# Mixture stage: GpSimd's bias addition at another unit, the output products over four units

## The chip, the core and the metric

The kernel runs on one core of a Trainium2 chip. The engines are TensorE (PE; its weight loads are shown apart as PEld), VectorE (DVE), ScalarE (ACT), GpSimd (POOL) and SyncE (SP), each with an instruction stream of its own; they wait for each other by semaphores. The metric is the device time of one execution in microseconds (us), the median of several runs.

## The reference, cut to what matters

Two transformer layers over 8 x 1024 tokens of width 256. Only the last part, the second layer's feed-forward, is touched: a mixture of 16 experts over 8 slices of 32 columns of each token.

```python
h = x @ Wm + bm
t = h.reshape(bs * L_ * H, HD)            # H = 8 slices, HD = 32
logits = t @ expert_emb
w = softmax(logits); topw, topi = top_k(w, 2)
hmid = gelu(einsum('td,edi->tei', t, W1) + b1)
eo = einsum('tei,eio->teo', hmid, W2) + b2
comb = (sel * topw[:, :, None]).sum(axis=1)   # the two chosen experts
out = comb.reshape(bs, L_, d)
return out @ Wo + bo                       # x + this is the result
```

The product with `Wo` is what is called the output product below, and `bo` is the bias that GpSimd adds to the residual tiles.

## The kernel before

`mixture_ffn` works through 16 blocks (m = 0 to 15) of 512 tokens, that is four tiles of 128 tokens each (t = 0 to 3). All experts are computed for all tokens, and gates that are zero for experts not chosen weigh them. A block has 32 units: `u = 16 * hc + e`, expert e on one half (hc) of the 8 slices. Each unit goes through a pipeline of four engines:

- PE `hidden` (L2010): four products of 512 columns into one of three pairs of banks, `HP`; a pair of them may start when ACT has emptied the pair that stood three pairs before.
- ACT (L2110): two gelus of 1024 elements for a unit.
- PE `expert_out` (L2020): the second product into the single bank `OP`. It waits for the gelus and for `y_ready`, that is until DVE has read the unit before.
- DVE `gate_unit` (L2207): adds the expert's bias, multiplies by the gates (`gates_spread`), and writes `gated` (two buffers), or `combined` itself where e is 0. It waits for `y_added`, so that POOL has finished with the buffer two units before.
- POOL `sum_up` (L2092): adds `gated` into `combined`. Where e is 0 it has nothing to add.

The order on every engine is written out by hand with tables that say what else a unit does. In unit u of block m, PE issues `hidden(u)`, `expert_out(u-1)`, then the output products of block m-1 that `OUTPUT_AT` names, then a piece of the front of block m+1 that `FRONT_AT` names. DVE follows with `gate_unit(u-1)`, the additions of those output products to the residual tiles (L2195), and its own pieces of the front. The front of the next block is: normalization `xn` (L2130) at units 0 and 1, two tiles each; transposes at units 2 to 5 (L1965, copied by L2135); the product with `Wm` at units 6 and 8 (L1971); logits at unit 10; maxima and the masks at 11 to 13; ACT's exponential after unit 14's gelus, with an activation table load before and after it; the reciprocal at 18 (L2172, L2174), gates at 19 and 20, and their transposes at 22. All products that are not `hidden` or `expert_out` share one bank, `MB` (`misc_bank`): each waits on `misc_free` until DVE has copied the one before.

POOL's stream for a block is one bias addition to the block's four residual tiles (L2081, 128 x 1024 elements) and then 30 additions of units. `let_front_pass` makes POOL's addition for unit u wait until a piece of the front that DVE does in unit u+1 is finished, for the pieces n, s, d, k and w; so the addition for unit 31 waits for the normalization at unit 0 of the next block. The bias addition has no such wait beyond one for the block's own normalization, which is long past except in block 0. DVE's first output addition of the block waits for it (`biased`).

The first block's front runs before the blocks; block 0 has no output products to issue, block 15 no front; the output products of block 15 come after the last unit. The two tables and the head of POOL's routine:

```python
FRONT_AT = dict(zip((0, 1, 2, 3, 4, 5, 6, 7, 8, 9, 10, 11, 12, 13, 18, 19, 20, 22), FRONT))
EXP_AT = 14
OUTPUT_AT = {15: (0, 1), 16: (2,), 17: (3,)}
```

Of the kernel before, what the change touches and what calls it, by code (L numbers as in the profile page):

```python
# [15 lines left out]
ALU = mybir.AluOpType  # L16
ACT = mybir.ActivationFunctionType
AX = mybir.AxisListType
P = 128
D = 256  # L20
# [1792 lines left out]
def mixture_ffn(nc, X, STATS, MEAN, RS, B, weights, out, ident):  # L1813
# [5 lines left out]
    TT = 4  # L1819
# [7 lines left out]
    with ExitStack() as ctx:  # L1827
# [3 lines left out]
        def sem(name):  # L1831
            return ctx.enter_context(nc.semaphore(name))

        wm, wo, w1s, w2, embd = weights.wm, weights.wo, weights.w1s, weights.w2, weights.embd
        bmc, b1c, b2c, bor = weights.bmc, weights.b1c, weights.b2c, weights.bor
# [31 lines left out]
        xn_ready = sem("xn2_ready")  # L1867
        biased = sem("biased2")
# [18 lines left out]
        ON_PE = "xhlg"  # L1887
        FRONT_AT = dict(zip((0, 1, 2, 3, 4, 5, 6, 7, 8, 9, 10, 11, 12, 13, 18, 19, 20, 22), FRONT))
        EXP_AT = 14
        OUTPUT_AT = {15: (0, 1), 16: (2,), 17: (3,)}  # L1890
        OUT_STORE_AT = 20
        STORE_AT = {5: (0,), 6: (1,)}
        LOAD_AT = {6: (0,), 7: (1,)}
# [64 lines left out]
        def _(pe):  # L1958
# [31 lines left out]
            def output(m, par, t, k):  # L1990
                if t == 0:
                    pe.wait_ge(y_added, NU * m + NU + 1)
                pe.wait_ge(misc_free, k + 1)
                for h in range(HC):
                    mm = nc.tensor.matmul(MB[:, 0:D], CM[:, par, h, t * P:(t + 1) * P], wo[:, h, :],  # L1995
                                          start=(h == 0), stop=(h == HC - 1))
                mm.then_inc(misc_done, 1)
# [16 lines left out]
            def expert_out(m, u):  # L2014
                hc, e = divmod(u, E)
                n = NU * m + u
                pe.wait_ge(y_ready, n + 1)
                pe.wait_ge(gelu_done, 2 * n + 2)
                for j in range(G):
                    mm = nc.tensor.matmul(OP[HD * j:HD * (j + 1), :], w2[:, e, :],  # L2020
                                          GH[:, (2 * u + j // 2) % 4, j % 2, :], start=True, stop=True,
                                          tile_position=(0, HD * j))
                mm.then_inc(o_done, 1)
# [3 lines left out]
            def one_block(m, par, first, last):  # L2027
                k = before(m)
                for u in range(NU):
# [5 lines left out]
                    elif not first:  # L2035
                        expert_out(m - 1, NU - 1)
                    for t in () if first else OUTPUT_AT.get(u, ()):
                        output(m - 1, 1 - par, t, k)
# [18 lines left out]
        @block.gpsimd  # L2057
        def _(pool):
            pool.sem_inc(y_added, 1)

            def let_front_pass(m, u):

                m, u = (m, u + 1) if u + 1 < NU else (m + 1, 0)
                if m >= NM - 1 or u not in FRONT_AT:
                    return
                part, t = FRONT_AT[u]
                if part == "n":
                    pool.wait_ge(xn_ready, TT * (m + 1) + 2 * t + 2)
                elif part == "s":
                    pool.wait_ge(slices_ready, HC * (m + 1) + t + 1)  # L2070
                elif part == "d":
                    pool.wait_ge(lm_ready, m + 2)
                elif part == "k":
                    pool.wait_ge(gates_kept, m + 2)
                elif part == "w":
                    pool.wait_ge(gates_ready, m + 2)

            def sum_up(m, par):
                pool.wait_ge(xn_ready, TT * (m + 1))
                xs = X[:, TT * m:TT * (m + 1), :]  # L2080
                nc.gpsimd.tensor_tensor(xs, xs, bor[:, :].unsqueeze(1).to_broadcast([P, TT, D]), ALU.add)\  # L2081
                  .then_inc(biased, 1)
                for u in range(NU):
                    hc, e = divmod(u, E)
                    n = NU * m + u
                    pool.wait_ge(y_ready, n + 2)
                    pool.wait_ge(y_added, n + 1)
                    if e == 0:
                        pool.sem_inc(y_added, 1)
                    else:  # L2090
                        let_front_pass(m, u)
                        nc.gpsimd.tensor_tensor(CM[:, par, hc, :], CM[:, par, hc, :], Y[:, u % 2, :], ALU.add)\  # L2092
                          .then_inc(y_added, 1)

            for m in range(NM):
                sum_up(m, m % 2)
# [27 lines left out]
        def _(dve):  # L2124
# [66 lines left out]
            def output(m, t, k):  # L2191
                if t == 0:
                    dve.wait_ge(biased, m + 1)
                dve.wait_ge(misc_done, k + 1)
                nc.vector.tensor_tensor(X[:, TT * m + t, :], X[:, TT * m + t, :], MB[:, 0:D], ALU.add)\  # L2195
                  .then_inc(misc_free, 1)

            def gate_unit(m, par, u):
                hc, e = divmod(u, E)
                n = NU * m + u  # L2200
                dve.wait_ge(o_done, n + 3)
                q, i = divmod(u, GE)
                if i == 0:
                    dve.wait_ge(gate_in[q % GGROUPS], 16 * G * (NG // GGROUPS * m + q // GGROUPS + 1))
                if e:
                    wait(dve, y_added, n)
                nc.vector.scalar_tensor_tensor(out=Y[:, u % 2, :] if e else CM[:, par, hc, :], in0=OP[:, :],  # L2207
                                               scalar=b2c[:, e:e + 1], in1=GS[:, q % GGROUPS, i, :], op0=ALU.add,
                                               op1=ALU.mult).then_inc(y_ready, 1)
# [4 lines left out]
            def one_block(m, par, first, last):  # L2214
                k = before(m)
                for u in range(NU):
                    if u >= 1:
                        gate_unit(m, par, u - 1)
                    elif not first:
                        gate_unit(m - 1, 1 - par, NU - 1)  # L2220
                    for t in () if first else OUTPUT_AT.get(u, ()):
                        output(m - 1, t, k)
# [34 lines left out]
def program(nc, a, out):  # L2257
    B = a["L0_attn_x"].shape[0]
    NT = B * KT
    with ExitStack() as ctx:  # L2260
        X = ctx.enter_context(nc.sbuf_tensor("x_tiles", [P, NT, D], F32))
        MEAN = ctx.enter_context(nc.sbuf_tensor("ln_mean", [P, NT], F32))
        RS = ctx.enter_context(nc.sbuf_tensor("ln_rstd", [P, NT], F32))
        STATS = ctx.enter_context(nc.sbuf_tensor("ln_stats", [P, NT, 6], F32))
        ident = ctx.enter_context(nc.sbuf_tensor("ident", [P, P], F32))
        identb = ctx.enter_context(nc.sbuf_tensor("ident_bf16", [P, P], BF16))
        make_idents(nc, ident, identb)
        causal_attention(nc, a["L0_attn_x"], X, STATS, MEAN, RS, B, a["L0_attn_Wq"], a["L0_attn_Wk"],
                         a["L0_attn_Wv"], ident, identb)
        expert_ffn(nc, X, STATS, MEAN, RS, B, *(a["L0_ffn_" + n] for n in (  # L2270
            "Wg", "bg", "Wu", "bu", "Wd", "bd", "Wq", "keys", "down_embed", "up_embed")), ident)
        later = MixtureWeights(nc, ctx, *(a["L1_ffn_" + n] for n in (
            "Wm", "bm", "expert_emb", "W1", "b1", "W2", "b2", "Wo", "bo")))
        rotary_attention(nc, X, STATS, MEAN, RS, B, *(a["L1_attn_" + n] for n in ("wq", "wk", "wv", "wo")),
                         a["rotation_cos"], a["rotation_sin"], ident, later)
        mixture_ffn(nc, X, STATS, MEAN, RS, B, later, out, ident)
# [32 lines left out]
```

## Time and profile before

| | us |
|---|---|
| median of 3 runs | 4446.77 (4442.31 to 4447.55) |
| the profiled execution | 4446.02 |
| its span, first to last instruction | 4444.3 |
| the mixture stage's blocks | from about 3138 to the end |
| one block in the middle of the stage | 80.88 |
| PE busy in such a block | 78.19 |
| ACT busy in such a block | 70.97 |
| DVE busy in such a block | 42.05 |
| POOL busy in such a block | 41.10 |

The rows further down are of four kinds. A row of busy time by stretch has the stretch in us from the span's start and its length, then the busy time and the count of instructions of PE, PEld, DVE, ACT and POOL, then TensorE's granted clock as a share of full speed, the busy share of the DMA engines and GB/s. A row of the chain of waits has a start, a length and the work. A row of waits has the waiting engine and line, the releaser, and total us, times and longest us. A row of the timeline has a start and a length in us, the engine, the line, what is written from what, shapes, and the number of instructions merged into it; in brackets stands how long the engine was idle before it and what ended that.

### The profile page before, as it was taken

Reading aid. Unit: us, or ns where it says so; the run is one execution under the profiler, and the core shown is the slowest. Engines: PE = TensorE matmul, PEld = TensorE weight load, DVE = VectorE, ACT = ScalarE, POOL = GpSimd, SP = SyncE. Lnnn points to the kernel's source line nnn. Section 1 sums busy time; section 2 is a strip of 40 time slices with the busy share of each in tenths; the row PEclk is TensorE's granted clock in tenths of the full one; section 3 lists DMA queues with packets and bytes.
Section 4 is the critical chain, followed back from the end, with each engine's and each line's share of the span. In section 5 each row is a group of like instructions: output and inputs, shape, how many; then the busy total and the mean of one; then the engine's idle time right before and its main releaser. Section 6 shows DMA issues by size and latency. Waiting matters only on the chain. (4 is left out here: it accounts for less than half of the span.)

```text
span 4444.3 us, 62551 instructions
## 1 busy us (share of the span) xinstructions
PE 4191.6 (94%) x22580; PEld 2204.3 (50%) x22580; DVE 2774.3 (62%) x5566; ACT 2654.1 (60%) x3193; POOL 1453.3 (33%) x1113
## 2 busy tenths in 40 slices
PE   7999999999978999999999998999899999999999
PEld 4444444444534566566565565555344444444443
DVE  6777777777748677677677655554455555554553
ACT  1555565565556454454454423444688888888888
POOL 3111111111125344343343322120354545545545
PEclk7999999999999999999999999999899999999999
DMA  7333433434210000000000001000766667666673
GB/s 174 83 95 81 101 75 79 97 91 84 60 56 1 0 1 1 1 1 1 1 1 1 0 1 33 1 1 1 165 140 163 154 140 164 152 151 162 140 163 92
DMA packets 145746, 322.79 MB, mean 73 GB/s; under 512 B 39296, under 2 KB 64272, under 8 KB 129056
## 3 DMA queue, kind: packets, MB, share of 16 engines
q1 hardware_dynamic: 137456, 310.88, 30.3%
q10 hardware_dynamic: 7920, 7.87, 0.6%
q8 instruction: 182, 2.98, 0.3%
q14 instruction: 124, 1.02, 0.1%
q0 software_dynamic: 64, 0.05, 0.0%
HBM read 237.93 MB, written 80.74 MB: 72 GB/s over the span
## 5 line engine op out<-in xcount | busy, mean ns | idle before, releaser
L2110 ACT ACTIVATE gelu_out<-hidden,b_col 128x1024 f32<-128x1024 f32 x1024 | 1084.2, 1112 | 160.8 <-PE hidden L2010 160.1
L648 DVE TENSOR_REDUCE maxima<-front 128x1 f32<-128x512 f32 (+3 forms) x1280 | 738.0, 631 | 175.5 <-PE front L458 101.6
L2092 POOL TENSOR_TENSOR combined<-combined,gated 128x512 f32<-128x512 f32 x480 | 619.6, 1291 | 664.7 <-DVE gated L2207 456.7
L550 ACT ACTIVATE probsT<-scoresT 128x1024 f32<-128x1024 f32 (+3 forms) x768 | 584.2, 812 | 305.7 <-PE scoresT L486 301.2
L1062 POOL TENSOR_TENSOR pair_sums<-sims 128x1024 f32<-128x1024 f32 x256 | 481.9, 1903 | 788.2 <-DVEq L1188 517.6
L2207 DVE SCALAR_TENSOR_TENSOR gated<-expert_out,b_col,gates_spread 128x512 f32<-128x512 f32 x480 | 360.0, 750 | 500.9 <-PE expert_out L2020 295.2
L2010 PE MATMUL hidden<-slice_stack,w_stack 128*128 128x512 f32 x2048 | 626.0, 427 | 15.0 <-ACT gelu_out L2110 15.0
L2020 PE MATMUL expert_out<-gelu_out,w_sb 128*32 128x512 f32 x4096 | 546.7, 606 | 24.7 <-DVE gated L2207 13.5
L2010 PEld LDWEIGHTS hidden<-slice_stack,w_stack 128*128 128x128 f32 x2048 | 351.4, 189 | 370.2 <-ACT gelu_out L2110 281.6
L399 POOL TENSOR_SCALAR_AFFINE_SELECT probsT<-probsT 128x512 f32<-128x512 f32 x256 | 163.4, 638 | 1078.7 <-ACT probsT L550 1078.7
L452 PE MATMUL front<-k_stack,q_stack 62*128 62x512 f32 (+3 forms) x1536 | 436.9, 429 | 34.8 <-DVE maxima L648 15.1
L452 PEld LDWEIGHTS front<-k_stack,q_stack 62*128 62x128 f32 x1536 | 216.9, 192 | 288.8 <-DVE maxima L648 183.9
L1117 ACT ACTIVATE pair_exp<-pair_sums,neg_max 128x1024 f32<-128x1024 f32 x256 | 284.5, 1116 | 120.4 <-DVE expert_weight L1218 114.2
L501 PE MATMUL pv<-probsT,values 128*32 128x512 f32 (+3 forms) x3072 | 332.4, 505 | 0.8 <-ACT outT L521 0.5
L1207 DVE SCALAR_TENSOR_TENSOR pair_exp<-pair_sums,top_pairs,pair_exp 128x1024 f32<-128x1024 f32 x256 | 322.3, 1281 | 11.1 <-ACT pair_exp L1117 10.9
L1194 DVE SCALAR_TENSOR_TENSOR hiddenT<-dense,bu_col,silu_gate 128x512 f32<-128x512 f32 x128 | 95.7, 750 | 366.0 <-PE dense L1012 366.0
L486 PE MATMUL scoresT<-q_stack,k_stack 64*128 64x512 f32 (+3 forms) x1536 | 304.6, 407 | 12.4 <-ACT probsT L550 9.5
L1100 ACT ACTIVATE silu_gate<-dense,bg_col 128x512 f32<-128x512 f32 x128 | 87.6, 687 | 305.2 <-PE dense L1004 305.1
L1218 DVE SCALAR_TENSOR_TENSOR expert_weight<-pair_exp,recip_z,expert_weight 128x1024 f32<-128x1024 f32 x192 | 246.5, 1284 | 8.4
L1004 PE MATMUL dense<-xnT,wg_sb 128*128 128x512 f32 x512 | 240.8, 592 | 2.2 <-ACT silu_gate L1100 2.1
L1012 PE MATMUL dense<-xnT,wu_sb 128*128 128x512 f32 x512 | 240.6, 592 | 0.0
L1028 PE MATMUL dense<-up_sb,silu_down 128*128 128x256 f32 x1024 | 231.8, 379 | 5.0 <-DVE silu_down L1243 5.0
(205 smaller groups left out, 5650.1 us busy)
## 6 DMA issues: line engine op xcount, KB each, us to landing
gates_spread<-gate_scratch SPq DMA_DIRECT2D x512, 256.0 KB, 4.8
stack_scratch<-split_parts SPq DMA_DIRECT2D x192, 256.0 KB, 3.0
slice_stack<-slice_scratch SPq DMA_DIRECT2D x128, 256.0 KB, 7.7
q_stack<-stack_scratch SPq DMA_DIRECT2D x64, 384.0 KB, 6.2
k_stack<-stack_scratch SPq DMA_DIRECT2D x64, 384.0 KB, 9.3
slice_scratch<-slice_parts SPq DMA_DIRECT2D x32, 512.0 KB, 6.2
out_x<-x_tiles ACTq DMA_DIRECT2D x15, 512.0 KB, 5.0
x_tiles<-in_L_attn_x SPq DMA_DIRECT2D x7, 1024.0 KB, 11.8
```

The costliest lines, as they stand in the source:

```text
L452: mm = nc.tensor.matmul(F[k % 3][:, a * w:at], QS[rows, hf, q, qt * P:(qt + 1) * P], KS[rows, hf, q, kc * BANK:kc * BANK + w], start=True, ...
L486: mm = nc.tensor.matmul(bank[:, e, at:BANK], KS[rows, hf, q, kt * P:(kt + 1) * P], QS[rows, hf, q, c * BANK + at:(c + 1) * BANK], start=Tr ...
L501: mm = nc.tensor.matmul(PV[32 * j:32 * (j + 1), at:BANK], V[:, n % 2, kt, (G * g + j) * HV:(G * g + j) * HV + 32], PT[:, i % NPT, j, at:BA ...
L550: nc.scalar.activation(PT[:, i % NPT, 2 * pr:2 * pr + 2, at:BANK], ST[pr][:, :, at:BANK], ACT.Exp, scale=SCALE).then_inc(probs_ready, 1)
L648: nc.vector.tensor_reduce(dst, F[k % 3][:, 0:parts * w].rearrange("p (a k) -> p a k", a=parts), AX.X, ALU.max)\
L1062: nc.gpsimd.tensor_tensor(A[:, h, :].rearrange("p (i j) -> p i j", i=NR), SM[:, m % 2, t, 0, h, 0:NR].unsqueeze(2).to_broadcast([P, NR, NK ...
L1207: nc.vector.scalar_tensor_tensor(out=E[h % 2][:, :], in0=A[:, h, :], scalar=T8[:, H * t + h, TOPK - 1:TOPK], in1=E[h % 2][:, :], op0=ALU.i ...
L2010: mm = nc.tensor.matmul(HP[k % HPB][:, j, :], w1s[:, e, :], HS[:, par, G * hc + 2 * p + j, :], start=True, stop=True)
L2020: mm = nc.tensor.matmul(OP[HD * j:HD * (j + 1), :], w2[:, e, :], GH[:, (2 * u + j // 2) % 4, j % 2, :], start=True, stop=True, tile_positi ...
L2092: nc.gpsimd.tensor_tensor(CM[:, par, hc, :], CM[:, par, hc, :], Y[:, u % 2, :], ALU.add)\
L2110: nc.scalar.activation(GH[:, k % 4, :, :], HP[k % HPB][:, :, :], ACT.Gelu, bias=b1c[:, u % E:u % E + 1])\
L2207: nc.vector.scalar_tensor_tensor(out=Y[:, u % 2, :] if e else CM[:, par, hc, :], in0=OP[:, :], scalar=b2c[:, e:e + 1], in1=GS[:, q % GGROU ...
```

## The change

Two places. POOL's bias addition for block m is no longer issued ahead of the block's units but just ahead of its 27th unit (u = 26, `BIAS_AT`), with the same wait and the same semaphore. And the output products of the four tiles, with DVE's additions that follow them, are issued one each at units 15, 16, 17 and 18, where they were two at 15 and one each at 16 and 17. No instruction is added or removed.

```diff
-        OUTPUT_AT = {15: (0, 1), 16: (2,), 17: (3,)}
+        BIAS_AT = 26
+        OUTPUT_AT = {15: (0,), 16: (1,), 17: (2,), 18: (3,)}
...
             def sum_up(m, par):
-                pool.wait_ge(xn_ready, TT * (m + 1))
-                xs = X[:, TT * m:TT * (m + 1), :]
-                nc.gpsimd.tensor_tensor(xs, xs, bor[:, :].unsqueeze(1).to_broadcast([P, TT, D]), ALU.add)\
-                  .then_inc(biased, 1)
                 for u in range(NU):
                     hc, e = divmod(u, E)
                     n = NU * m + u
+                    if u == BIAS_AT:
+                        pool.wait_ge(xn_ready, TT * (m + 1))
+                        xs = X[:, TT * m:TT * (m + 1), :]
+                        nc.gpsimd.tensor_tensor(xs, xs, bor[:, :].unsqueeze(1).to_broadcast([P, TT, D]), ALU.add)\
+                          .then_inc(biased, 1)
                     pool.wait_ge(y_ready, n + 2)
                     pool.wait_ge(y_added, n + 1)
```

POOL's stream at a border between two blocks, before (the additions for units 19 to 31, then the bias addition of the next block, then its unit 1):

```order
L2092 TENSOR_TENSOR combined<-combined,gated 128x512 [waits gates_ready,y_added,y_ready]
L2092 TENSOR_TENSOR combined<-combined,gated 128x512 [waits y_added,y_ready] x11
L2092 TENSOR_TENSOR combined<-combined,gated 128x512 [waits xn2_ready,y_added,y_ready]
L2081 TENSOR_TENSOR x_tiles<-x_tiles,bo_rows 128x1024 [waits xn2_ready]
L2092 TENSOR_TENSOR combined<-combined,gated 128x512 [waits y_ready,y_added]
```

The same place in the changed kernel (its L2094 is L2092 of before, L2086 is L2081):

```order
L2094 TENSOR_TENSOR combined<-combined,gated 128x512 [waits gates_ready,y_added,y_ready]
L2094 TENSOR_TENSOR combined<-combined,gated 128x512 [waits y_added,y_ready] x6
L2086 TENSOR_TENSOR x_tiles<-x_tiles,bo_rows 128x1024 [waits xn2_ready]
L2094 TENSOR_TENSOR combined<-combined,gated 128x512 [waits y_added,y_ready] x5
L2094 TENSOR_TENSOR combined<-combined,gated 128x512 [waits xn2_ready,y_added,y_ready]
L2094 TENSOR_TENSOR combined<-combined,gated 128x512 [waits y_ready,y_added]
```

The bias addition has moved from between units 31 and 1 to between units 25 and 26. No wait has gone or come.

PE's stream in units 15 to 19, from the `expert_out` issued in unit 15, before (L1995 is an output product, two instructions for a tile):

```order
L2020 MATMUL expert_out<-gelu_out,w_sb 32x512 x4
L1995 MATMUL misc_bank<-wo_sb,combined 128x256 x4
L2010 MATMUL hidden<-slice_stack,w_stack 128x512 x4
L2020 MATMUL expert_out<-gelu_out,w_sb 32x512 x4
L1995 MATMUL misc_bank<-wo_sb,combined 128x256 x2
L2010 MATMUL hidden<-slice_stack,w_stack 128x512 x4
L2020 MATMUL expert_out<-gelu_out,w_sb 32x512 x4
L1995 MATMUL misc_bank<-wo_sb,combined 128x256 x2
L2010 MATMUL hidden<-slice_stack,w_stack 128x512 x4
L2020 MATMUL expert_out<-gelu_out,w_sb 32x512 x4
L2010 MATMUL hidden<-slice_stack,w_stack 128x512 x4
```

The same stretch in the changed kernel (L1996, L2011 and L2021 are L1995, L2010 and L2020 of before):

```order
L2021 MATMUL expert_out<-gelu_out,w_sb 32x512 x4
L1996 MATMUL misc_bank<-wo_sb,combined 128x256 x2
L2011 MATMUL hidden<-slice_stack,w_stack 128x512 x4
L2021 MATMUL expert_out<-gelu_out,w_sb 32x512 x4
L1996 MATMUL misc_bank<-wo_sb,combined 128x256 x2
L2011 MATMUL hidden<-slice_stack,w_stack 128x512 x4
L2021 MATMUL expert_out<-gelu_out,w_sb 32x512 x4
L1996 MATMUL misc_bank<-wo_sb,combined 128x256 x2
L2011 MATMUL hidden<-slice_stack,w_stack 128x512 x4
L2021 MATMUL expert_out<-gelu_out,w_sb 32x512 x4
L1996 MATMUL misc_bank<-wo_sb,combined 128x256 x2
L2011 MATMUL hidden<-slice_stack,w_stack 128x512 x4
```

In unit 15 one tile's output product follows `expert_out` where there were two, and unit 18, which had none, has the fourth tile's.

## Rows read from the trace of the kernel before

**Rows 1.** Busy time by stretch, block 1 to 2; columns are explained above
```profile
3321.47:3402.35 80.88, 78.19 (x437) 33.87 (x437) 42.05 (x90) 70.97 (x68) 41.10 (x31) 1.00 0.66 152
```

**Rows 2.** Chain of waits, the same product (unit 6) in blocks 0, 1, 2
```profile
3161.45 1.91 PE misc_bank L1971 x4
...
3240.60 1.91 PE misc_bank L1971 x4
...
3321.47 1.91 PE misc_bank L1971 x4
```

**Rows 3.** Waits on PE, blocks 1 to 14: us in total, times, longest
```profile
PE expert_out L2020 <- DVE gated L2207: 12.6, 14, 0.9
```

**Rows 4.** Timeline, units 1 to 5 of block 4; columns are explained above
```profile
3471.68 2.88 DVE L2130 TENSOR_SCALAR xn<-x_tiles,ln_mean,ln_rstd 128x256 f32<-128x256 f32 x2
3471.71 2.38 POOL L2081 TENSOR_TENSOR x_tiles<-x_tiles,bo_rows 128x1024 f32<-128x1024 f32 x1
...
3473.20 1.18 PE L2010 MATMUL hidden<-slice_stack,w_stack 128*128 128x512 f32 x4
...
3475.28 1.06 PE L2020 MATMUL expert_out<-gelu_out,w_sb 128*32 128x512 f32 x8 [0.90 <-DVE gated L2207]
...
3476.47 1.18 PE L2010 MATMUL hidden<-slice_stack,w_stack 128*128 128x512 f32 x4
...
3478.76 1.18 PE L2010 MATMUL hidden<-slice_stack,w_stack 128*128 128x512 f32 x4
```

**Rows 5.** Timeline, unit 0 of block 5, normalization with no bias addition beside it
```profile
3550.44 0.73 DVE L2130 TENSOR_SCALAR xn<-x_tiles,ln_mean,ln_rstd 128x256 f32<-128x256 f32 x2
```

**Rows 6.** Timeline, units 15 to 20 of block 4
```profile
3509.40 4.13 ACT L2110 ACTIVATE gelu_out<-hidden,b_col 128x1024 f32<-128x1024 f32 x4
...
3511.67 1.06 PE L2020 MATMUL expert_out<-gelu_out,w_sb 128*32 128x512 f32 x8 [0.36 <-ACT gelu_out L2110]
...
3513.44 1.28 PE L2010 MATMUL hidden<-slice_stack,w_stack 128*128 128x512 f32 x4
...
3516.43 1.28 PE L2010 MATMUL hidden<-slice_stack,w_stack 128*128 128x512 f32 x4
...
3516.82 0.42 DVE L2195 TENSOR_TENSOR x_tiles<-x_tiles,misc_bank 128x256 f32<-128x256 f32 x1 [0.28 <-PE misc_bank L1995]
...
3518.64 1.20 PE L2010 MATMUL hidden<-slice_stack,w_stack 128*128 128x512 f32 x4
...
3520.19 0.35 DVE L2174 RECIPROCAL gate_recip<-gate_recip 128x32 f32<-128x32 f32 x1
...
3520.76 1.20 PE L2010 MATMUL hidden<-slice_stack,w_stack 128*128 128x512 f32 x4
3520.90 0.75 DVE L2207 SCALAR_TENSOR_TENSOR gated<-expert_out,b_col,gates_spread 128x512 f32<-128x512 f32 x1 [0.35 <-POOL combined L2092]
```

**Rows 7.** Timeline of PE, unit 16 of block 0, no output products
```profile
3188.79 0.74 PE L2010 MATMUL hidden<-slice_stack,w_stack 128*128 128x512 f32 x2 [2.33 <-ACT gelu_out L2110]
3189.89 1.06 PE L2020 MATMUL expert_out<-gelu_out,w_sb 128*32 128x512 f32 x8 [0.36 <-ACT gelu_out L2110]
```

**Rows 8.** Timeline, late units of block 4
```profile
3541.23 1.28 POOL L2092 TENSOR_TENSOR combined<-combined,gated 128x512 f32<-128x512 f32 x1 [0.85 <-DVE gated L2207]
...
3542.52 0.75 DVE L2207 SCALAR_TENSOR_TENSOR gated<-expert_out,b_col,gates_spread 128x512 f32<-128x512 f32 x1 [1.37 <-POOL combined L2092]
...
3544.65 0.75 DVE L2207 SCALAR_TENSOR_TENSOR gated<-expert_out,b_col,gates_spread 128x512 f32<-128x512 f32 x1 [1.37 <-POOL combined L2092]
```

**Rows 9.** Timeline, unit 0 of block 15, bias addition beside a gating instruction
```profile
4360.61 2.40 POOL L2081 TENSOR_TENSOR x_tiles<-x_tiles,bo_rows 128x1024 f32<-128x1024 f32 x1
4360.66 0.75 DVE L2207 SCALAR_TENSOR_TENSOR combined<-expert_out,b_col,gates_spread 128x512 f32<-128x512 f32 x1 [1.37 <-PE expert_out L2020]
```

**Rows 10.** Timeline of PE, unit 15 of block 15
```profile
4390.25 1.13 PE L1995 MATMUL misc_bank<-wo_sb,combined 128*128 128x256 f32 x4
4391.96 1.13 PE L1995 MATMUL misc_bank<-wo_sb,combined 128*128 128x256 f32 x4 [0.58 <-DVE x_tiles L2195]
```

## The prediction, made before the changed kernel ran

> **What bounds the kernel now.** I read the chain of waits first. From 3138 us on it is PE work almost alone, and the same product comes back in it every 80.87 us; from block 0 to block 1 it is 79.15 [rows 2]. A block is thus a fixed cycle, and a step counts if it lengthens that cycle. The busy time by stretch says how tight the cycle is: PE is busy 78.19 of 80.88 us, ACT 70.97, DVE and POOL about half, and the granted clock is 1.00, the upper of the two levels, 2.4 GHz [rows 1]. So DVE and POOL matter only where one of them makes PE or ACT late at a certain unit. The timeline then shows where. An ordinary unit takes 2.12 us (the gating instructions of two units in a row start at 3542.52 and 3544.65) [rows 8], about the time of its two gelus: four of them take 4.13 us [rows 6]. A unit with a transpose takes 2.29 (3476.47 to 3478.76) [rows 4]. Two places stand out, and the change touches both: units 2 to 3, and units 15 to 17.
>
> **Part 1: the bias addition leaves the block's start.** At unit 1 DVE normalizes two tiles and POOL starts the bias addition in the same moment. The pair of normalizations takes 2.88 us [rows 4]; at unit 0 the same pair takes 0.73 [rows 5]. DVE is held for 2.15 us, nearly the 2.38 us of the addition. The next gating instruction queues behind the normalization on DVE, and `expert_out` waits for that one: PE is idle for 0.90 us before it, and the unit lasts 3.27 us (3473.20 to 3476.47) where the next lasts 2.29, a loss of 0.98 us [rows 4]. The waits on PE have this 14 times, 12.6 us in all [rows 3]: in the starts of blocks 1 to 14. Block 0's bias addition ran in the prologue, beside nothing that it held, and block 15 has no normalization beside it.
>
> With the addition gone from there POOL has nothing between the additions for units 31 and 1, so nothing can hold the normalization. The gating instruction then waits for `expert_out` alone, as in other units, and the unit falls to its neighbours' 2.29. The next thing that is late there is PE itself. **Term 1: 14 x 0.98 = 13.7 us less.**
>
> **Part 1, the other end: the addition in unit 26.** No piece of the front lies in units 23 to 31, so DVE does only gating there. Two things could cost time.
>
> (a) The addition could hold a gating instruction as it held the normalization. In these units an addition of POOL ends (3541.23 + 1.28 = 3542.51) when the next gating instruction starts (3542.52) [rows 8], so the bias addition will start together with a gating instruction and cover it. The trace has just this case: in block 15 the bias addition runs from 4360.61 to 4363.01 and the gating instruction that starts at 4360.66 takes 0.75 us, as everywhere [rows 9]. Nothing is held. Here the Trainium skill speaks against the change: its page "SBUF — State Buffer", section "SBUF: two separate sides", says that a VectorE instruction in a two-port mode or with two SBUF inputs and a GpSimd instruction exclude each other for the whole instruction. The gating instruction reads the gates and the bias column from SBUF, and if the column counts as the second input it would be held in unit 26. That is a rival below; rows 9 speak against it, and by them the price is nothing.
>
> (b) The additions behind it are late. Bias addition 2.38 and addition of unit 26 1.28, from 3542.51 in the frame of rows 8, end at 3546.2. Who waits for it is the gating of unit 28, two gating starts later, at 3542.52 + 2 x 2.12 = 3546.77. That leaves some 0.5 us, and from there POOL, with 1.28 us of work for a unit of 2.12, catches up. Cost taken: nothing; cover: 0.5 us of slack, plus what PE has behind DVE.
>
> Where the addition's end is awaited (DVE's first output addition, a dozen units into the next block) it is early in either place.
>
> **Part 2: the output products.** What do the four products cost now? Block 0 has none, and from its unit 6 to the next block's it takes 79.15 us; the next stretch, with four products, takes 80.87 [rows 2]. Four products cost 1.72 us together. In units 16 and 17, the hidden products start 2.99 us apart (3513.44 to 3516.43) where ordinary units take 2.12 [rows 6], so each of these two costs 0.87, and 2 x 0.87 = 1.74 is already all of it: **the two products in unit 15 are free.** The reason is in the same rows: ACT, which has loaded its table for the exponential and loaded gelu's again, starts the gelus of unit 15 only at 3509.40, and `expert_out` in unit 16 waits for the second of them until 3511.67, idle for 0.36 before [rows 6]. In block 0, without products, PE is idle for 2.33 us in that place [rows 7]. Both products fit into that gap.
>
> So taking one product out of unit 15 brings nothing in blocks 1 to 14: `expert_out` of unit 16 still waits for the same gelu. The product of tile 1 goes to unit 16 and that of tile 2 to 17, where others stood, and the fourth goes to unit 18. Units 18 and 19 (hidden products at 3516.43, 3518.64, 3520.76) take 2.21 and 2.12 [rows 6]; the 2.21 is the echo of the product before it. ACT has no lead there that could hide a product. I take for unit 18 what units 16 and 17 pay, 0.87. **Term 2: 14 x 0.87 = 12.2 us more.** Bounds: nothing, if unit 18 had a gap, and 0.35 more if DVE became late. On DVE the fourth output addition stands ahead of the reciprocal pair, which now ends at 3520.54. An output addition waits 0.28 and takes 0.42 [rows 6], so the pair ends 0.70 later, at 3521.24, and the next gating instruction, due at 3520.90 + 0.87 = 3521.77, has 0.5 us to spare. The wait of 0.35 before it goes. Hence no extra.
>
> Block 15 has no exponential, so no gap in unit 15. There the second product starts 1.71 us after the first, with a wait of 0.58 for DVE to empty the bank [rows 10]. Moved to a unit of its own, it costs 0.87: **Term 3: 1.71 - 0.87 = 0.84 us less**, once.
>
> The shorter work of PE in unit 15 leaves it idle for about 2.33 less one product's 0.87, some 1.5 us. Block 0's 2.33 us of idle were followed by `expert_out` at 1.06 us, the ordinary time [rows 7], so the clock stays up.
>
> **The sum.** -13.7 + 12.2 - 0.8 = -2.4 us. A middle block goes from 80.88 to 80.77. Against the profiled execution's own 4446.02 that is 4443.6; the median of the runs, 4446.77, less 2.4 is 4444.4. I say **4444**.
>
> **Rivals.**
>
> *The fourth product is free as well* (faster). If PE had a gap in unit 18, or the freed 0.98 us early in the block gave ACT a lead that lasts, term 2 would go: -13.7 - 0.8 = -14.5, 4431.5 us. For it: the change shortens the crowd in unit 15. Against it: units 18 and 19 already run at the gelus' pace with no idle time, and the table loads end any lead.
>
> *The gap in units 2 to 3 stays* (slower). The hold of the normalization could come from POOL's addition for unit 31, which stands right ahead of the bias addition on POOL, or the 0.90 us could have another cause that only now shows. Then term 1 is nothing: 4446.0 + 12.2 - 0.8 = 4457.4. Against it: at unit 0 there is no bias addition and the pair takes 0.73.
>
> *The gating instruction is held in unit 26* (much slower). Place: the gating that starts with the bias addition; price: up to the addition's 2.38 us, in 16 blocks, up to 38 us on top of 4443.6, so up to 4482. It decides from the point where that instruction takes more than 0.75 us, or where the additions behind come over 0.5 us later than in (b). Rows 9 exclude it as far as one case can.
>
> **How the numbers follow.** Forecast 0.84; fourth product free 0.07; gap stays 0.06; gating held 0.03. The range takes the forecast with its bounds: upward 14 x 0.35 = 4.9 us, 4448.5, and a little for the spread of the runs (5 us from lowest to highest), 4450; downward half of term 2 and the spread, 4436. It leaves the three rivals out, 0.16 together. About 0.2%, 8.9 us, is what a measurement can tell from no change: faster means below 4437.9, slower above 4455.7. Faster: 0.07 and 0.02 of the forecast, 0.09. Slower: 0.06 + 0.03, 0.09. Same: the other 0.82.
>
> **What would show it.** Step 1: the normalization pair at unit 1 takes 0.73 to 0.8, and the 14 waits of `expert_out` for the gating, 12.6 us, are gone. Step 1b: bias additions between units 25 and 26, gating instructions at 0.75 throughout, hidden products 2.12 apart in units 24 to 31. Step 2: three units of 2.99 (16, 17 and 18) in place of two, the gelus of unit 15 and `expert_out` behind them no earlier relative to the block, PE idle over 1 us in unit 16 before its second pair. The block 80.77 long; block 15 shorter by 0.8. I would be wrong if unit 18 stayed near 2.12, if a gating instruction near the bias addition took over 0.75, or if the first units kept a unit of 3.27.

## The result, and the profile after

The changed kernel takes 4459.25 us (median of 8 runs, 4451.48 to 4464.62), the kernel before 4446.5 (8 runs, 4442.0 to 4449.72). The ratio is 1.003, 95% interval 1.002 to 1.0039: **slower by 0.3%, 12.8 us**, where 4444 was forecast, with 4450 as the upper end. Its runs also lie wider apart, 13 us where the kernel before has 8.

The chain of waits of the changed kernel, the same product in unit 6 of blocks 1 to 5 (start, length, work), to be read beside [rows 2]:

```profile
3242.86 1.91 PE misc_bank L1972 x4
...
3323.64 1.91 PE misc_bank L1972 x4
...
3404.41 1.91 PE misc_bank L1972 x4
...
3486.78 1.91 PE misc_bank L1972 x4
...
3569.20 1.92 PE misc_bank L1972 x4
```

The blocks are no longer alike. Two take 80.78 and 80.77 us, to the hundredth what was forecast, and the next two 82.37 and 82.42. Of the 13 such stretches from block 1 to block 14, seven last 80.77 or 80.78 us and six 82.31 to 82.42; with block 14's own there are seven long blocks: 3, 4, 8, 10, 11, 13 and 14.

PE in units 15 to 17 of block 4, a long block (columns as in the timeline of before: start, length, engine, line, work, instructions, idle time before it):

```profile
3511.05 1.13 PE L1996 MATMUL misc_bank<-wo_sb,combined 128*128 128x256 f32 x4
3511.83 0.82 PE L2011 MATMUL hidden<-slice_stack,w_stack 128*128 128x512 f32 x2
3514.12 0.73 PE L2011 MATMUL hidden<-slice_stack,w_stack 128*128 128x512 f32 x2 [1.47 <-ACT gelu_out L2112]
3515.22 1.67 PE L2021 MATMUL expert_out<-gelu_out,w_sb 128*32 128x512 f32 x8 [0.36 <-ACT gelu_out L2112]
3516.82 2.08 PE L1996 MATMUL misc_bank<-wo_sb,combined 128*128 128x256 f32 x4
3518.33 1.57 PE L2011 MATMUL hidden<-slice_stack,w_stack 128*128 128x512 f32 x4
...
3521.61 1.28 PE L2011 MATMUL hidden<-slice_stack,w_stack 128*128 128x512 f32 x4
```

The same place in block 5, a short one:

```profile
3594.24 0.82 PE L2011 MATMUL hidden<-slice_stack,w_stack 128*128 128x512 f32 x2
3596.53 0.74 PE L2011 MATMUL hidden<-slice_stack,w_stack 128*128 128x512 f32 x2 [1.47 <-ACT gelu_out L2112]
3597.63 1.07 PE L2021 MATMUL expert_out<-gelu_out,w_sb 128*32 128x512 f32 x8 [0.36 <-ACT gelu_out L2112]
...
3599.41 1.28 PE L2011 MATMUL hidden<-slice_stack,w_stack 128*128 128x512 f32 x4
...
3602.39 1.28 PE L2011 MATMUL hidden<-slice_stack,w_stack 128*128 128x512 f32 x4
```

Up to `expert_out` (L2021) the two are the same: one output product (L1996), half of `hidden`, 1.47 us idle for ACT, the other half, 0.36 us idle. Then `expert_out` takes 1.67 us instead of 1.07 and the next output product 2.08, where that of unit 15 took 1.13. From the second half of `hidden` to the `hidden` of unit 18 it is 7.49 us against 5.86: 1.63 us lost. The six long stretches exceed the others by 1.54 to 1.65 us. The busy time by stretch of the long block says why (stretch and length; busy time of PE, PEld, DVE, ACT, POOL; granted clock; DMA share; GB/s):

```profile
3512.00:3515.50 3.50, 1.67 (x9) 0.68 (x11) 0.42 (x1) 3.49 (x4) 1.28 (x1) 1.00 1.06 289
3515.50:3519.00 3.50, 3.50 (x13) 1.83 (x6) 0.82 (x2) 1.58 (x2) 1.24 (x1) 0.51 0.78 156
```

For one stretch of about 3.4 us the granted clock is 0.51, the lower of the two levels, 1.2 GHz, and before it PE was busy for 1.67 of 3.5 us. In the kernel before no such stretch lies in blocks 1 to 14; here there are seven, one in each long block, and each begins in this place, between 28.4 and 29.3 us behind the start of the block's product of unit 6. Below, such a stretch of half clock in unit 16, or just ahead of it, is called a fall.

A thin PE is not the whole of it. In the same 3.5 us of block 5 (3594.41 to 3597.91) PE is busy for 1.67 too, and the granted clock stays at 1.00. In the kernel before, the same place of block 4 has two output products, an idle time of 0.58 us between them and none before `hidden`, and PE is busy for 2.56 of 3.5 us:

```profile
3509.21 1.13 PE L1995 MATMUL misc_bank<-wo_sb,combined 128*128 128x256 f32 x4 [0.58 <-DVE x_tiles L2195]
3509.99 1.32 PE L2010 MATMUL hidden<-slice_stack,w_stack 128*128 128x512 f32 x4
```

and, by stretch, with the columns as above,

```profile
3508.45:3511.95 3.50, 2.56 (x13) 1.54 (x16) 0.84 (x2) 3.49 (x4) 1.27 (x1) 1.00 1.06 269
```

The rest of the change went as its parts were meant. DVE and POOL at the block's start, where [rows 4] had 2.88 us for the pair of normalizations:

```profile
3474.08 0.73 DVE L2132 TENSOR_SCALAR xn<-x_tiles,ln_mean,ln_rstd 128x256 f32<-128x256 f32 x2
3475.55 0.75 DVE L2209 SCALAR_TENSOR_TENSOR combined<-expert_out,b_col,gates_spread 128x512 f32<-128x512 f32 x1 [0.73 <-PE expert_out L2021]
3476.21 0.73 DVE L2132 TENSOR_SCALAR xn<-x_tiles,ln_mean,ln_rstd 128x256 f32<-128x256 f32 x2
3477.67 0.75 DVE L2209 SCALAR_TENSOR_TENSOR gated<-expert_out,b_col,gates_spread 128x512 f32<-128x512 f32 x1 [0.73 <-PE expert_out L2021]
```

Both pairs take 0.73, and the 14 waits of `expert_out` for the gating, 12.6 us [rows 3], are gone: among the waits on PE in blocks 1 to 14 only ACT is left. The first row below holds 14 waits of 1.47 us in unit 16 and 13 of 0.84 us near the block's end, which the kernel before has too.

```profile
PE hidden L2011 <- ACT gelu_out L2112: 31.5, 27, 1.5
PE expert_out L2021 <- ACT gelu_out L2112: 5.0, 14, 0.4
```

And the bias addition in its new place, unit 26 of block 4, with the gating beside it and hidden products 2.12 us apart:

```profile
3544.27 2.40 POOL L2086 TENSOR_TENSOR x_tiles<-x_tiles,bo_rows 128x1024 f32<-128x1024 f32 x1
...
3546.32 1.20 PE L2011 MATMUL hidden<-slice_stack,w_stack 128*128 128x512 f32 x4
3546.45 0.75 DVE L2209 SCALAR_TENSOR_TENSOR gated<-expert_out,b_col,gates_spread 128x512 f32<-128x512 f32 x1 [1.37 <-PE expert_out L2021]
3546.61 4.16 POOL L2094 TENSOR_TENSOR combined<-combined,gated 128x512 f32<-128x512 f32 x3
...
3548.44 1.20 PE L2011 MATMUL hidden<-slice_stack,w_stack 128*128 128x512 f32 x4
```

The gating takes 0.75 us as everywhere; POOL's next three additions run in a row (4.16 us), and nobody waits for them.

The profiled execution took 4459.2 us with a span of 4457.5, against 4446.02 and 4444.3 before. The 13.2 us between the spans are made of:

| | us |
|---|---|
| units 2 and 3 of blocks 1 to 14, 14 x 0.98 | -13.7 |
| fourth product in unit 18 of blocks 1 to 14, 14 x 0.87 | +12.2 |
| block 15, from its unit 15 to 20: 14.07 us instead of 14.92 | -0.85 |
| half clock in unit 16 of seven blocks, 7 x 1.63 | +11.4 |
| first of the last output products at half clock, 2.07 instead of 1.13 | +0.94 |
| ahead of the mixture stage, whose code is the same | +3.2 |
| sum | +13.2 |

The 3.2 us ahead of the stage belong to no change: the stage's first transpose starts at 3113.31 us where it was 3110.01, and over the ten profiles of this document, whose code up to there is the same, it starts between 3106.1 and 3113.9.

### The profile page after: what moved, and what is told of

Same layout as the page of the kernel before. It is cut to its first block and busy times, and to the rows that moved or that the text cites. A ratio compares the mean times of both kernels' runs of the same rounds, so it can differ in the third digit from the quotient of the medians.

```text
span 4457.5 us, 62551 instructions
## 1 busy us (share of the span) xinstructions
PE 4204.3 (94%) x22580; PEld 2212.0 (50%) x22580; DVE 2745.8 (62%) x5566; ACT 2653.1 (60%) x3193; POOL 1450.6 (33%) x1113
## 5 line engine op out<-in xcount | busy, mean ns | idle before, releaser
L2094 POOL TENSOR_TENSOR combined<-combined,gated 128x512 f32<-128x512 f32 x480 | 618.9, 1289 | 734.6 <-DVE gated L2209 509.7
L2011 PE MATMUL hidden<-slice_stack,w_stack 128*128 128x512 f32 x2048 | 633.5, 430 | 35.5 <-ACT gelu_out L2112 35.5
L2021 PE MATMUL expert_out<-gelu_out,w_sb 128*32 128x512 f32 x4096 | 550.2, 609 | 12.0 <-ACT gelu_out L2112 5.7
L2011 PEld LDWEIGHTS hidden<-slice_stack,w_stack 128*128 128x128 f32 x2048 | 354.9, 190 | 383.3 <-ACT gelu_out L2112 293.0
```

Of the source, the lines that this page charges most:

```text
L2011: mm = nc.tensor.matmul(HP[k % HPB][:, j, :], w1s[:, e, :], HS[:, par, G * hc + 2 * p + j, :], start=True, stop=True)
```

## The experiments

Theory 1: the single output product of unit 15 leaves PE too thin in the time in which it waits for ACT's table loads, and TensorE's clock falls behind that wait. Theory 2: the bias addition in unit 26 costs, by itself or through the clock. All times are medians beside the kernel before on the same chip.

### Each part alone

The bias addition moved, the products as before (against the changed kernel):

```diff
-        OUTPUT_AT = {15: (0,), 16: (1,), 17: (2,), 18: (3,)}
+        OUTPUT_AT = {15: (0, 1), 16: (2,), 17: (3,)}
```

> The bias addition in unit 26, the output products as before (two in unit 15, one each in 16 and 17). Theory 1 (the thinner unit 15 lets TensorE's clock fall behind the wait for the gelus): this part alone is a pure gain, 14 x 0.98 = 13.7 us, about 4432.5, blocks of 79.90 us, no stretch of half clock in blocks 1 to 14. Theory 2 (the bias addition beside the gating in unit 26 is what costs, by its own time or by the clock): not faster than before, 4446 or more, and half-clock stretches or units over 2.12 us near unit 26.

Measured: 4431.6 us (4428.07 to 4437.58, 8 runs) beside 4444.37 of before, ratio 0.9971 (0.996 to 0.9981). Unit 6 of blocks 1 and 2 in the chain of waits:

```profile
3241.81 1.91 PE misc_bank L1972 x4
...
3321.72 1.91 PE misc_bank L1972 x4
```

79.91 us, and all 13 such stretches last 79.90 to 79.92. There is no half clock in blocks 1 to 14. **The first part alone makes the kernel faster by 12.8 us**, and theory 2 is out.

The products moved, the bias addition at the block's start (against the kernel before):

```diff
-        OUTPUT_AT = {15: (0, 1), 16: (2,), 17: (3,)}
+        OUTPUT_AT = {15: (0,), 16: (1,), 17: (2,), 18: (3,)}
```

> The output products one each in units 15 to 18, the bias addition at the block's beginning. Theory 1: about seven blocks of 14 lose 1.6 us to half clock in unit 16, and the fourth product costs 0.87 in each: 4446 + 12.2 - 0.8 + 7 to 9 x 1.63, about 4470; the unit of 3.27 us is back. Theory 2: blocks of 81.75 us and no half clock, about 4457.

Measured: 4460.67 us (4456.71 to 4461.29, 5 runs), ratio 1.0032 (1.0019 to 1.0046). Blocks without a fall last 81.73 to 81.75 us, the forecast 81.75; in the profiled run three of blocks 1 to 14 (1, 5 and 14) hold a fall, and the stretches of the first two last 83.3. So the clock falls with the products alone, but three times where I had expected seven to nine: the median is 9 us under my figure. The wait is the same as with the whole change. In block 1, where the clock fell:

```profile
3266.79 0.73 PE L2010 MATMUL hidden<-slice_stack,w_stack 128*128 128x512 f32 x2 [1.46 <-ACT gelu_out L2110]
3267.89 1.14 PE L2020 MATMUL expert_out<-gelu_out,w_sb 128*32 128x512 f32 x8 [0.36 <-ACT gelu_out L2110]
3268.97 2.08 PE L1995 MATMUL misc_bank<-wo_sb,combined 128*128 128x256 f32 x4
3270.48 2.06 PE L2010 MATMUL hidden<-slice_stack,w_stack 128*128 128x512 f32 x4
```

How thin PE is in that place bears on whether the clock can fall; it does not alone decide how often.

### PE given more to do in the wait

The changed kernel, where in blocks 1 to 14 the product of unit 15 is computed twice over, into the same place:

```diff
+                for again in range(2 if t == 0 and m < NM - 2 else 1):
+                    for h in range(HC):
...
-                for h in range(HC):
```

> The changed kernel, but in unit 15 of blocks 1 to 14 the one output product is done twice over (four matmul instructions in place of two, the same result): TensorE does more work in the place where two products stood before. Theory 1: the added work lies in the wait for the gelus and costs nothing, the idle time before the second half of hidden falls from 1.47 to about 0.7 us, no half clock in blocks 1 to 14, all blocks 80.77 us, about 4443.5, so faster than the changed kernel by more than 10 us. Rival: if the clock has another cause, the time stays at about 4459, or rises by up to 14 x 0.78 = 11 us.

Measured: 4443.65 us (4440.48 to 4449.42, 10 runs), ratio 0.9998 (0.9989 to 1.0008), and not one stretch of half clock in the blocks. PE in units 15 and 16 of block 4:

```profile
3503.62 1.99 PE L1997 MATMUL misc_bank<-wo_sb,combined 128*128 128x256 f32 x8
3505.26 0.82 PE L2012 MATMUL hidden<-slice_stack,w_stack 128*128 128x512 f32 x2
3506.69 0.74 PE L2012 MATMUL hidden<-slice_stack,w_stack 128*128 128x512 f32 x2 [0.61 <-ACT gelu_out L2113]
3507.78 1.06 PE L2022 MATMUL expert_out<-gelu_out,w_sb 128*32 128x512 f32 x8 [0.36 <-ACT gelu_out L2113]
```

The idle time is down from 1.47 to 0.61 us, and `expert_out` starts no later against the gelus (0.36 idle before it, as ever). All blocks from the first on last 80.76 to 80.78. Work that nobody needs makes the changed kernel faster by more than 10 us, and it lands where the prediction had put the changed kernel, at 4443.6.

With half of that filler, one matmul instruction more than the changed kernel (the timeline counts each of these instructions as two, so 6 where there were 4):

```diff
+                for hs in ((0,), range(HC)) if t == 0 and m < NM - 2 else (range(HC),):
+                    for h in hs:
...
-                for h in range(HC):
```

> The changed kernel with one matmul instruction more in unit 15 (three in place of two; the second filler had four): PE's idle time falls from 1.47 to about 1.1 us. Theory 1: fewer falls of the clock than with the change, between none and four of 14 blocks, 4443.5 to 4452. If only a full product's work keeps the clock up, as many falls as with the change: about 4459.

Measured: 4443.91 us (4440.54 to 4446.58, 10 runs), ratio 0.9993 (0.9984 to 1.0003). The wait:

```profile
3506.97 1.56 PE L1997 MATMUL misc_bank<-wo_sb,combined 128*128 128x256 f32 x6
3508.19 0.82 PE L2012 MATMUL hidden<-slice_stack,w_stack 128*128 128x512 f32 x2
3510.05 0.73 PE L2012 MATMUL hidden<-slice_stack,w_stack 128*128 128x512 f32 x2 [1.04 <-ACT gelu_out L2113]
3511.14 1.07 PE L2022 MATMUL expert_out<-gelu_out,w_sb 128*32 128x512 f32 x8 [0.36 <-ACT gelu_out L2113]
```

1.04 us idle, and no fall in any block (80.76 to 80.78 us throughout). I had left room for up to four. Some 0.4 us of matmul work in that place separate seven falls, or the five of the second profile below, from none.

### Less to do in the wait, and no wait at all

The products in units 16 to 19, none in 15:

```diff
-        OUTPUT_AT = {15: (0,), 16: (1,), 17: (2,), 18: (3,)}
+        OUTPUT_AT = {16: (0,), 17: (1,), 18: (2,), 19: (3,)}
```

> The changed kernel with the four products in units 16, 17, 18 and 19, none in 15: the idle time before the second half of hidden grows from 1.47 to about 2.3 us. Without any fall of the clock a block is 81.6 us and the kernel 4443.6 + 13 = 4456.5. Theory 1: half clock in at least as many blocks as with the change (7 of 14), rather in most of them: 4468 to 4480. Rival (idle time is not what counts; block 0 had 2.33 us of it twice without a fall): no more falls than with the change, 4456 to 4468.

Measured: 4470.68 us (4469.67 to 4476.64, 4 runs), ratio 1.006 (1.0045 to 1.0075). Blocks without a fall last 81.63 or 81.64 us. Nine of blocks 1 to 14 hold falls (2, 3, 4, 7, 8, 9, 12, 13 and 14), and block 0 too; blocks 2, 7 and 12 hold one twice as long and last 84.1. One such block:

```profile
3518.51 0.74 PE L2011 MATMUL hidden<-slice_stack,w_stack 128*128 128x512 f32 x2
3521.58 1.22 PE L2011 MATMUL hidden<-slice_stack,w_stack 128*128 128x512 f32 x2 [2.33 <-ACT gelu_out L2112]
3522.73 1.94 PE L2021 MATMUL expert_out<-gelu_out,w_sb 128*32 128x512 f32 x8
```

2.33 us idle, and here already the second half of `hidden` runs at half clock, 1.22 us instead of 0.74. The fall is as frequent as theory 1 wanted, and no longer confined to what follows the wait. Block 0 is the very place of [rows 7], with the same code and the same 2.33 or 2.34 us of idle time, and here the granted clock is 0.50 (3193.50 to 3196.80): `expert_out` takes 1.94 us (at 3194.70) where [rows 7] has 1.06.

The wait itself taken away: ACT computes a square in place of the exponential, and the trace has no table load beside it. The gates, and with them the result, are then not the reference's.

```diff
-                nc.scalar.activation(EX[:, :, :, :], LM[:, :, :, :], ACT.Exp).then_inc(ex_ready, 1)
+                nc.scalar.activation(EX[:, :, :, :], LM[:, :, :, :], ACT.Square).then_inc(ex_ready, 1)
```

> The changed kernel with ACT's exponential replaced by a square, which needs no table load (the gates are then not the reference's): the cause of TensorE's wait is gone, not the wait filled. Theory 1: the idle time of 1.47 us in unit 16 goes, no half clock in blocks 1 to 14, a block is 80.77 - 2.17 = 78.60 us (the stretch from hidden to expert_out of unit 15 falls to block 15's 4.12 from 6.29), about 4413. Rival (the falls come from something else in the new order): half clock stays in some blocks, 1.6 us each, about 4425.

Measured: 4411.76 us (4407.61 to 4414.36, 4 runs), ratio 0.992 (0.9905 to 0.9935), all blocks 78.59 or 78.60 us, no half clock in blocks 1 to 14. PE goes straight from the output product to the whole of `hidden` and to `expert_out`:

```profile
3499.12 1.13 PE L1996 MATMUL misc_bank<-wo_sb,combined 128*128 128x256 f32 x4
3499.90 1.28 PE L2011 MATMUL hidden<-slice_stack,w_stack 128*128 128x512 f32 x4
3501.11 1.06 PE L2021 MATMUL expert_out<-gelu_out,w_sb 128*32 128x512 f32 x8
```

With the order of the changed kernel but without the wait nothing falls. The table loads cost a block 2.17 us here, 30 us in blocks 1 to 14 together.

### The changed kernel once more

> The changed kernel once more, beside the others on one chip. Theory 1: falls of the clock again, each in unit 16, in a number that differs from run to run, so a median between 4451 and 4465 and a spread wider than before's; blocks without one are 80.77 us again. If the falls of the first profile were a chance of one chip: about 4443.6 and none.

Measured: 4457.08 us (4444.45 to 4461.96, 10 runs) beside 4445.55 (4441.64 to 4450.45, 19 runs), ratio 1.0023 (1.0014 to 1.0032). Its profiled run took 4451.05 us and has five falls, in blocks 8, 10, 11, 13 and 14, all in unit 16; the other blocks last 80.76 to 80.78. By the sum, 4443.6 + 5 x 1.63 = 4451.8. One of the ten runs, 4444.45, is as fast as if the clock had not fallen at all. The mean granted clock of the single runs goes the same way: 0.978 in the run of 4444.45, as in most runs of the kernel before, and 0.974 in that of 4461.96. So the number of falls is what spreads the changed kernel's times, as far as a mean over the whole run can show it.

### A version that fills the wait with needed work

If 2.3 us of PE's time are free in that place, all four output products should go there. A second pair of products needs a second bank; `expert_out`'s is free between DVE's gating of unit 14 and `expert_out` of unit 15. Each pair fills a bank and DVE adds it in one instruction; the bias addition stays in unit 26. PE's part of the edit (DVE's additions, the stores and the semaphore counts are adapted to pairs, not shown):

```diff
-        OUTPUT_AT = {15: (0,), 16: (1,), 17: (2,), 18: (3,)}
+        OUTPUT_AT = {15: (0, 1)}
...
+                else:
+                    pe.wait_ge(y_ready, NU * (m + 1) + (16 if m < NM - 1 else 1))
+                bank = OP if t else MB
+                for i in range(2):
+                    for h in range(HC):
+                        mm = nc.tensor.matmul(bank[:, D * i:D * i + D], CM[:, par, h, (2 * t + i) * P:(2 * t + i + 1) * P],
+                                              wo[:, h, :], start=(h == 0), stop=(h == HC - 1))
...
+                    if u - 1 == max(OUTPUT_AT) and not first:
+                        pe.wait_ge(misc_free, k + 1)
```

> A version that uses the wait for the gelus in unit 15 in full: bias addition in unit 26, and all four output products in unit 15, two tiles into the bank of the front's products and two into expert_out's bank (free there between the gating of unit 14 and expert_out of unit 15), each pair with one DVE addition of 128 x 512. If two products in unit 15 are free because PE waits there for 2.33 us, four products (4 x 0.78 = 3.1 us) overrun it by little and the 1.74 us a block that two products still cost go: blocks of 78.2 to 78.5 us, 4404 to 4409 us, no half clock in blocks 1 to 14. If DVE's reading of the second bank makes expert_out late, each block keeps up to 1 us of it: up to 4420.

Measured: **4410.05 us** (4406.41 to 4413.19, 4 runs) beside 4445.55, ratio 0.9917 (0.9902 to 0.9931): 0.8% faster than the kernel before and the best of all. No half clock in blocks 1 to 14. Units 15 and 16 of a block:

```profile
3495.76 1.99 PE L2002 MATMUL misc_bank<-wo_sb,combined 128*128 128x256 f32 x8
...
3497.60 1.89 PE L2002 MATMUL expert_out<-wo_sb,combined 128*128 128x256 f32 x8
3497.67 2.12 ACT L2120 ACTIVATE gelu_out<-hidden,b_col 128x1024 f32<-128x1024 f32 x2
...
3499.14 1.28 PE L2017 MATMUL hidden<-slice_stack,w_stack 128*128 128x512 f32 x4
3499.52 0.69 DVE L2207 TENSOR_TENSOR x_tiles<-x_tiles,expert_out 128x512 f32<-128x512 f32 x1 [0.97 <-PE expert_out L2002]
3499.99 9.61 ACT L2120 ACTIVATE gelu_out<-hidden,b_col 128x1024 f32<-128x1024 f32 x9 [0.20 <-PE hidden L2017]
...
3500.34 1.07 PE L2027 MATMUL expert_out<-gelu_out,w_sb 128*32 128x512 f32 x8
```

The eight matmuls that the timeline counts for each pair follow each other, ACT starts its gelus at 3497.67 in the middle of them, and its idle time is 0.20 us. The price of the second bank is there too: `expert_out` starts only when DVE has read it, at 3500.34, 0.55 us after the end of the first two gelus. A block lasts 78.61 us (3235.70 to 3314.31, unit 6 of blocks 1 and 2 in the chain of waits) where I had put 78.2 to 78.5. Of the 1.74 us that two products cost, 1.3 are gained (79.91 with the bias addition moved alone, 78.61 here).

## Why the prediction was wrong

**What held.** Term 1 was right: 0.98 us in each of 14 blocks, shown by the blocks of 79.91 us with the bias addition moved alone, forecast by the same working at 79.90. The addition in unit 26 costs nothing: the gating beside it takes 0.75 us and PE's pace stays at 2.12. So the row of block 15 [rows 9] was the right guide for the rival of the held gating. The Trainium skill (page "SBUF — State Buffer", section "SBUF: two separate sides") says that a VectorE instruction with two SBUF inputs and a GpSimd instruction that reads SBUF exclude each other for the whole instruction. The 0.75 us agree with it if the bias column is not counted as an input, and not if it is. Term 2 was right to the hundredth, 0.87 for the product in unit 18 (blocks of 81.75 us against 80.88 with the products moved alone), with the reciprocal pair behind it making nothing late, and term 3 was 0.85 for 0.84. A block without a fall of the clock lasts 80.77 us as forecast, and the changed kernel with the falls prevented 4443.65.

**What failed.** One sentence of part 2: "Block 0's 2.33 us of idle were followed by `expert_out` at 1.06 us, the ordinary time [rows 7], so the clock stays up." The row was read rightly and proves nothing. In the version without a product in unit 15 the same wait in the same place of block 0 was followed by `expert_out` at 1.94 us. The row is one wait in one place of one execution, and what it stands for happens in some blocks and not in others: with 1.47 us idle the clock fell in seven, five and three of 14 blocks in three profiles, and blocks 4 and 5 of the changed kernel, alike up to the wait's end, part there. With 2.33 us idle in every block it fell in nine of 14. I priced at nothing what costs about 1.6 us each time, 11.4 us of the profiled execution, and gave it no share of the range and no rival of its own. From the 4443.6 of the sum to the 4459.2 of that execution it is 15.6 us, and the rest of them is the half clock at the kernel's end (0.94) and the later start of the stage (3.2). The rival at 4457.4, by which the fourth product would cost its 12.2 us with nothing gained, has almost the measured time, but by a mechanism that did not happen: the gap in units 2 to 3 did go.

**The step behind it.** I called two products in unit 15 free because they lie in a wait, and concluded that taking one out "brings nothing". It brings a loss: in the kernel before these products were what kept PE busy through the wait (0.58 us idle instead of 1.47). That the wait has to be filled, and with how little, is shown by the two fillers; that it is the wait and not the new order, by the version without table loads.

**What stays open.** Why the clock falls in just these blocks. The falls are not scattered. From block 8 on both profiles of the changed kernel have the same sequence of lengths to 0.02 us (82.3, 80.8, 82.4, 82.4, 80.8, 82.4) and a fall in block 14, although the one had falls in blocks 3 and 4 and the other none before block 8. Without a product in unit 15 the lengths come back every five blocks (from block 2 on 84.1, 83.1, 82.5, 81.6, 81.6, then the same again). And with blocks of 81.75 us there are fewer falls than with blocks of 80.77, although the wait is as long. That suggests that it matters when in the chip's own time the wait comes. No run here varies that alone, so it is only argued.

## What to carry to other kernels

Work that lies free in an engine's wait may still be worth its place: here it kept TensorE's clock up, and moving one product out of the wait cost more than the rest of the change gained. Before you call a gap harmless, count over many gaps of that length and over several executions, not at one; a widened spread of the times is a sign. And where a wait can't be avoided, put into it all the needed work that fits, here four output products. That kernel is 35 us under the one before; some 13 us of it are the bias addition's, as in the run with that part alone, and the rest comes from the four products in the wait.

## What the runs showed of the hardware

- TensorE's granted clock fell from 1.00 to about 0.5 for 3.4 us behind a stretch in which PE was busy for 1.67 of 3.5 us, with single idle times of 1.47 and 0.36 us. A fall costs 1.54 to 1.65 us in the changed kernel. Of 14 such places the clock fell in seven, five and three in the three profiles that have them, and the same 1.67 of 3.5 us in another block left it at 1.00. With idle times of 1.04 and 0.61 us (the two fillers) it fell in none of 28, and with 0.58 us (the kernel before, and the bias addition moved alone) in none of 28 either.
- A GpSimd addition of two SBUF tensors over 1024 columns (2.38 to 2.40 us) stretches a pair of VectorE normalizations from SBUF to SBUF from 0.73 to 2.88 us, and leaves a VectorE instruction with one input in PSUM, one tensor and one bias column in SBUF at 0.75 us.
